# Drains of GpSimd's queue inside the program of a one-core decoder layer

## The chip, the cores and the metric

One core of one Trainium2 chip runs the whole layer. The metric is device time in microseconds (us), the median of several runs.

## The reference

A decoder layer with post-normalisation on x of 16 batches x 256 tokens x 256 features, float32. Cut to what matters:

```python
x = layernorm(x + attn(x, W_qkv, W_out))             # 16 heads, segments of 128 tokens, every 2nd key
x = layernorm(x + xattn(x, ctx, Wq, ..., Wo, bo))    # 16 heads, 77 keys of the context
logits = x @ router_w; e = argmax(logits); g = softmax(logits)[e]        # 14 experts, one per token
y = g * (gelu(x @ w1[e] + b1[e]) @ w2[e] + b2[e])
x = layernorm(x + y)
```

## The kernel before

Each engine runs a program of its own whose order is written out by hand as strings of steps (`POOL_FIRST`, `POOL_ORDER`, `POOL_LAST`, `POOL_TILES` for GpSimd and the like for the others). `step@lag` in `*_ORDER` is repeated for every two batches, `step:b` is one step of batch b, and `*_TILES` is repeated for every expert tile. Engines meet at semaphores.

The attention stage goes over the 16 batches. In it GpSimd scales the softmax's probabilities (`scale`, L1498), computes the layer norms' rstd (L1456, L1461) and masked keys (L1508, L1530), and does part of the routing. A pair of batches, p = b // 2 from 0 to 7, is 512 tokens. Once per pair, `pool_enter` writes them into the experts' lists in DRAM: four indirect DMAs of 128 entries each (L1579, "list entries"). From pair 2 on a small add to the tokens' numbers stands in front of them (L1572, "member step"), for which the first entry waits.

The expert stage goes over 45 tiles of 128 list rows. For tile j, SyncE loads the list's rows (`slots`, L722) and the expert's bias (L732), GpSimd gathers the tokens' rows by an indirect DMA (`pool_gather`, L1599, into a ring of six buffers), TensorE transposes them (`rows`, L740), makes the hidden layer (`hid`, L956) and the output (`y`, L972), VectorE adds bias (L1401) and residual (L1413) and takes statistics, GpSimd raises the variance to -0.5 (`pow`, L1613, "rs step"), VectorE normalises (L1436, "norm"), and GpSimd writes the rows to the output by an indirect DMA (`pool_put`, L1605, "put"). Tiles 0 to `NEARLY` - 1 = 10 hold tokens of the first 12 batches and start while the last batches are still in work; tiles from 11 on need the lists of all pairs.

In a steady tile the order is

```python
PE_TILES = "y@2 hid@0 rows@-1"
DVE_TILES = "eps@1 bias@0 wd@-4 res@0 stat@0 norm@1 agg@0"
POOL_TILES = "gather@-3 pow@3 put@4"
```

so that gather j is followed by pow j - 6 and put j - 7. At the change of stage `POOL_LAST` ends with `gather:6 r_less_max0:15 r_count_tile1:15 r_count_tile2:15 r_count_tile3:15 pow:0 enter0:13 gather:7 enter0:15`: the entries of pairs 6 and 7 with gather 7 between them, and behind them pow 1, put 0 and gather 8.

At the end GpSimd waits until the last four puts have landed. Then each engine's program closes with a DRAIN and a barrier of all engines, which the profile puts down to L100.

Of the kernel before, what the change touches and what calls it, by code (L numbers as in the profile page):

```python
# [48 lines left out]
def wait(eng, sig, b, k=None, held="", part=""):  # L49

    if isinstance(b, int) and b < 0 or held in HELD or f"{held}:{part}" in HELD:
        return
    eng.wait_ge(sig.sem, sig.at(b, k))


def decoder_layer(nc, x, x_cols, xk_cols, ctx_cols, w_qkv, w_out, wq, bq, wk, bk, wv, bv, wo, bo, router_w, w1, b1, w2,
# [19 lines left out]
    NTILE = NT + E - 1  # L76
# [4 lines left out]
    NEARLY = EARLY * TPB - (E - 1)  # L81
# [18 lines left out]
    with ExitStack() as top:  # L100
# [216 lines left out]
        def wait_ring(eng, ring, j, held=""):  # L317

            wait(eng, ring[j % len(ring)], j // len(ring), None, held)

        def exists(b):
            return not isinstance(b, int) or 0 <= b < B
# [238 lines left out]
        def phase_of(j):  # L561
            return int(j >= NEARLY)
# [25 lines left out]
        def settled(eng):  # L588

            eng.sem_inc(carried.sem, 1)  # L590
# [944 lines left out]
        def pool_routing(pool):  # L1535
            for what, k, b in in_order(POOL_FIRST, POOL_ORDER, POOL_LAST, POOL_TILES):
                if what == "scale":
                    pool_scale(pool, *unit_of(k, b))
                elif what == "kxblk":
                    pool_kxblk(pool, b)  # L1540
                elif what == "x1r":
                    pool_x1r(pool, b)
                elif what == "kblk":
                    pool_kblk(pool, b)
                elif what == "enter":
                    pool_enter(pool, b)
                elif what[:2] == "r_":
                    pool_route(pool, what[2:], k, b)
                elif what == "clear":
                    pool_clear(pool)  # L1550
                elif what == "gather":
                    pool_gather(pool, b)
                elif what == "put":
                    pool_put(pool, b)
                elif what == "pow":
                    pool_pow(pool, b)
                else:
                    pool_rstd(pool, int(k[0]), int(k[1]), b)

        def pool_enter(pool, b):  # L1560

            if not exists(b):
                return
            p = b // 2
            if p < 2:
                pool.sem_inc(token_stepped.sem, 1)
                pool.wait_ge(lists_filled.sem, lists_filled.at(0))
            else:
                for t in range(TPP):
                    wait(pool, entered[p % 2][t], p // 2 - 1, held="pool_enter.1", part=t)  # L1570
                settled(pool)
                nc.gpsimd.tensor_tensor(member_no[:, p % 2], member_no[:, p % 2], pair_step[:], ALU.add).then_inc(  # L1572
                    token_stepped.sem, 1)
            for t in range(TPP):
                if t == 0:
                    wait(pool, routed["place"], p, held="pool_enter.2")
                    wait(pool, routed["gate"], p, held="pool_enter.3")
                    wait(pool, token_stepped, p, held="pool_enter.4")
                nc.gpsimd.indirect_dma_start(lists, bass.IndirectOffsetOnAxis(ap=place_i[:, p % 2, t:t + 1], axis=0),  # L1579
                                             member[:, p % 2, t, :], None, bounds_check=LIST_ROWS - 1,  # L1580
                                             oob_is_err=False).then_inc(entered[p % 2][t].sem, 16)

        def pool_clear(pool):
# [2 lines left out]
                wait(pool, computed[job], B - 1)  # L1586
            nc.gpsimd.memset(xg[:].rearrange("p m d -> p (m d)"), 0.0).then_inc(rows_cleared.sem, 1)

        def pool_gather(pool, j):
            if j == 0:  # L1590
                pool.wait_ge(rows_cleared.sem, 1)
            if j in (0, NEARLY):
                for t in range(TPB):
                    for n in range(2):
                        wait(pool, x2_stored[n][t], PLANNED[phase_of(j)] // 2)
            wait(pool, f["res_done"], j - XR, held="pool_gather.1")
            wait_ring(pool, slots_loaded, j, held="pool_gather.2")
            rows = (B if phase_of(j) else EARLY) * S
            nc.gpsimd.indirect_dma_start(xg[:, j % XR, :], None, x2_dram[0:rows],  # L1599
                                         bass.IndirectOffsetOnAxis(ap=slots_no[:, j, 0:1], axis=0),  # L1600
                                         bounds_check=rows - 1, oob_is_err=False).then_inc(gathered[j % XR].sem, 16)
# [106 lines left out]
```

## Time and profile before

| | us |
|---|---|
| median of 3 runs | 639.02 (635.59 to 640.14) |
| span of the profiled execution, first to last instruction | 595.6 |
| TensorE busy in it | 563.3 (95%) |
| VectorE | 463.4 (78%) |
| ScalarE | 343.1 (58%) |
| GpSimd | 405.4 (68%) |
| GpSimd's indirect DMAs | 45 gathers, 45 puts, 32 list entries |

No time of its own is given for the profiled execution beyond its span; the median of the runs is 43.4 us above that. In the rows PE is TensorE's matmuls, DVE VectorE, ACT ScalarE, POOL GpSimd, SP SyncE; a q behind the name is the engine's queue (its sequencer), which waits and issues. A number such as L1599 is the line of the kernel. Behind an operation, in brackets, stands the idle time of its engine in front of it and what ended it; "issue" is time in which it waited for nothing that the profile shows.

### The profile page before, as it was taken

To read this page: it belongs to the slowest core of one execution; us is meant where nothing else is said; L and a number is where in the kernel's file an instruction comes from. 1 tells how busy PE (TensorE), PEld (TensorE's weight loads), DVE (VectorE), ACT (ScalarE), POOL (GpSimd) and SP (SyncE) were. 2 spreads that over 40 slices of the span, in tenths; PEclk is the share of its full clock that TensorE was granted. 3 is DMA by queue.
4 is the path that set the end of the run, shared out by engine and by line. 5 is a ranking of instruction groups with operands and counts; after the bars stand their busy time and mean duration, and the time that the engine had idled before them with its cause. 6 is when DMAs were issued, how large, how long until landed. Compare 5 with 4: busy or idle time off the path is not lost.

```text
span 595.6 us, 16640 instructions
## 1 busy us (share of the span) xinstructions
PE 563.3 (95%) x5608; PEld 476.7 (80%) x5608; DVE 463.4 (78%) x1071; ACT 343.1 (58%) x842; POOL 405.4 (68%) x554
## 2 busy tenths in 40 slices
PE   7989999999999999999999999799979999999990
PEld 6777788788888788788788778568869999999990
DVE  2779999999999899999999989865455566555561
ACT  1456666666676576665766766546625555555540
POOL 4346675678778678677678766776777677777652
PEclk9799999999999999999999999969989999999996
DMA  7415125125414314413714201114273333333200
GB/s 207 149 42 181 24 51 194 28 68 147 76 47 150 76 50 109 132 33 89 168 26 136 68 7 41 32 39 119 55 102 97 90 81 89 96 92 91 68 16 0
DMA packets 76692, 50.11 MB, mean 84 GB/s; under 512 B 39222, under 2 KB 70970, under 8 KB 76608
## 3 DMA queue, kind: packets, MB, share of 16 engines
q1 hardware_dynamic: 71264, 40.60, 26.8%
q0 software_dynamic: 5344, 8.44, 5.6%
q8 instruction: 47, 0.77, 0.6%
q14 instruction: 37, 0.30, 0.3%
HBM read 40.55 MB, written 10.60 MB: 86 GB/s over the span
## 4 chain that ended last, share of the span: by engine, by line
PE 74%; POOL 9%; issue 7%; DVE 5%; ACT 2%; DMA 1%; POOLq 0%; ACTq 0%; DVEq 0%
PE ps_r L822 15%; PE ps_r L740 13%; PE ps_s L956 10%; PE ps_r L972 10%; PE ps_r L807 5%; PE ps_r L902 5%; PE ps_s L762 4%; PE ps_s L753 3%; POOL token_lists L1579 3%; PE ps_r L795 2%; POOL prob L1498 2%; PE ps_r L879 2%; PE ps_r L897 2%; PE ps_r L904 2%; POOL out L1605 1%
## 5 line engine op out<-in xcount | busy, mean ns | idle before, releaser
L1498 POOL TENSOR_TENSOR prob<-prob,rden 128x616 f32<-128x616 f32 (+1 forms) x96 | 138.3, 1447 | 58.3 <-DVE rden L1173 56.6
L999 ACT COPY probT<-ps_r 128x512 f32<-128x512 f32 x192 | 86.8, 480 | 43.3 <-PE ps_r L740 41.4
L1141 DVE TENSOR_REDUCE mx<-ps_s 128x8 f32<-128x616 f32 (+1 forms) x96 | 88.8, 925 | 21.7 <-PE ps_s L753 14.9
L1019 ACT ACTIVATE prob<-prob 128x616 f32<-128x616 f32 (+1 forms) x96 | 79.4, 833 | 33.9 <-DVE prob L1152 33.9
L1161 DVE TENSOR_REDUCE den<-prob 128x8 f32<-128x616 f32 (+1 forms) x96 | 88.3, 921 | 6.9 <-ACT prob L1019 5.7
L1152 DVE TENSOR_TENSOR prob<-ps_s,mx 128x616 f32<-128x616 f32 (+1 forms) x96 | 89.8, 936 | 4.5 <-PE ps_r L740 3.0
L740 PE MATMUL ps_r<-ident,prob 128*128 128x128 f32 (+1 forms) x576 | 88.4, 281 | 1.6 <-POOL prob L1498 1.0
L956 PEld LDWEIGHTS ps_s<-xgT,w1b 128*128 128x128 f32 x720 | 87.2, 192 | 2.4 <-issue 0.3
L972 PE MATMUL ps_r<-w2s,hT 128*128 x360 | 86.7, 385 | 1.3 <-DVE yb L1401 1.1
L956 PE MATMUL ps_s<-xgT,w1b 128*128 128x128 f32 x720 | 87.9, 275 | 0.2 <-ACT xgT L1107 0.2
L740 PEld LDWEIGHTS ps_r<-ident,prob 128*128 128x128 f32 (+1 forms) x576 | 66.1, 142 | 16.8 <-issue 9.6
L972 PEld LDWEIGHTS ps_r<-w2s,hT 128*128 128x128 f32 x360 | 66.0, 193 | 9.3 <-issue 1.9
L1599 POOL DMA_INDIRECT xg<-x_rows,slots x45 | 47.4, 1053 | 33.8 <-DVE ys L1413 26.2
L585 DVE COPY w1b<-w1s 128x512 f32 x45 | 20.1, 447 | 55.2 <-PE ps_s L956 52.8
L1119 ACT ACTIVATE hT<-ps_s,b1t 128x128 f32<-128x128 f32 x180 | 51.4, 368 | 15.6 <-issue 12.1
L1107 ACT COPY xgT<-ps_r 128x256 f32<-128x256 f32 x45 | 16.7, 373 | 65.8 <-PE ps_r L740 65.8
L1605 POOL DMA_INDIRECT out<-yo,slots x45 | 47.4, 1053 | 8.7 <-issue 8.5
L1579 POOL DMA_INDIRECT token_lists<-member,place_i x32 | 32.4, 1013 | 13.5 <-issue 8.2
L762 PE MATMUL ps_s<-kxblk,qxT 32*128 32x154 f32 x512 | 35.2, 344 | 4.3 <-DVE prob L1152 4.3
L1461 POOL TENSOR_TENSOR rstd<-ve,neg_half 128x1 f32<-128x1 f32 x64 | 35.5, 554 | 5.0
L807 PE MATMUL ps_r<-probT,vX 128*32 128x128 f32 (+1 forms) x1024 | 37.9, 281 | 0.2 <-issue 0.2
L902 PE MATMUL ps_r<-wo_s,oTx 128*128 128x272 f32 x128 | 37.2, 414 | 0.1
(158 smaller groups left out, 1011.0 us busy)
## 6 DMA issues: line engine op xcount, KB each, us to landing
w1s<-in_w SPq DMA_DIRECT2D x14, 512.0 KB
w2s<-in_w SPq DMA_DIRECT2D x14, 512.0 KB
b2r<-in_b SPq DMA_DIRECT2D x45, 128.0 KB, 3.2
xT<-in_x_cols SPq DMA_DIRECT2D x16, 256.0 KB, 2.9
xres<-in_x SPq DMA_DIRECT2D x16, 256.0 KB
x_rows<-x2s SPq DMA_DIRECT2D x32, 128.0 KB, 1.9
xkT<-in_xk_cols SPq DMA_DIRECT2D x16, 128.0 KB, 2.7
ctxT<-in_ctx_cols SPq DMA_DIRECT2D x16, 77.0 KB, 2.1
```

The source lines that it names most:

```text
L740: return nc.tensor.transpose(dst, src, ident[:])
L807: last = nc.tensor.matmul(dst[32 * g:32 * g + 32, 0:P], vX[0:rows, b % 2, c, h, off:off + 32], probT[0:rows, par, c * P:(c + 1) * P], star ...
L822: last = nc.tensor.matmul(dst[:, 0:width], lhs(c), rhs(c), start=(c == 0), stop=(c == KC - 1))
L902: nc.tensor.matmul(dst[:, 0:DR], oTx[:, c, cols], wo_s[:, c, :], start=(c == 0), stop=False)
L956: last = nc.tensor.matmul(ps_s[:, j % 2, u * P:(u + 1) * P], w1b[:, j % 2, c, u * P:(u + 1) * P], xgT[:, j % 2, c * P:(c + 1) * P], start= ...
L972: last = nc.tensor.matmul(dst[:, 0:D], hT[:, j % 2, c, :], w2s[:, bass.ds(e, 1), c, :].rearrange("p a f -> p (a f)"), start=(c == 0), stop ...
L999: nc.scalar.copy(probT[0:rows, par, first:last], src[0:rows, 0:last - first]).then_inc(pT_copied[kind].sem, 1)
L1019: nc.scalar.activation(prob[:, n % 3, 0:width], prob[:, n % 3, 0:width], ACT.Exp, scale=SCALE).then_inc(exp_done[kind].sem, 1)
L1141: nc.vector.tensor_reduce(m, s, axis=AX, op=ALU.max).then_inc(max_done[kind].sem, 1)
L1152: nc.vector.tensor_tensor(p, s, mb, ALU.subtract).then_inc(sub_done[kind].sem, 1)
L1161: nc.vector.tensor_reduce(den[:, par, 0:heads], prob[:, n % 3, 0:heads * width].rearrange("p (h k) -> p h k", k=width), axis=AX, op=ALU.ad ...
L1498: nc.gpsimd.tensor_tensor(p, p, rden[:, par, 0:heads, None].to_broadcast([P, heads, width]), ALU.mult).then_inc(scaled[kind].sem, 1)
```

## The change

Two drains are put into GpSimd's program. One stands in front of everything that `pool_enter` does for a pair, except for pair 0: seven drains, for pairs 1 to 7. The other stands in front of the waits of a gather, for the tiles in `range(NEARLY + 4, NTILE, 6)`: gathers 15, 21, 27, 33 and 39. Nothing else is added, removed or moved.

```diff
@@ pool_enter
             p = b // 2
+            if p:
+                nc.gpsimd.drain()
             if p < 2:
                 pool.sem_inc(token_stepped.sem, 1)
@@ 
+        RETIRED_BEFORE = range(NEARLY + 4, NTILE, 6)
+
         def pool_gather(pool, j):
@@ 
                         wait(pool, x2_stored[n][t], PLANNED[phase_of(j)] // 2)
+            if j in RETIRED_BEFORE:
+                nc.gpsimd.drain()
             wait(pool, f["res_done"], j - XR, held="pool_gather.1")
```

The steps around the two drains at the change of stage, on GpSimd, in the program before (xg is the buffer of the gathers, member the tokens' numbers, token_lists the lists; the last gather of the first row is gather 6):

```order
328 L1599 DMA xg<-x2_rows,slots 128x256 x3
329 L1470 TENSOR_TENSOR ldif<-logits,lmax 128x56
330 L1487 TENSOR_TENSOR before<-before,onehot 128x14 x3
331 L1613 TENSOR_TENSOR rs<-ve,neg_half 128x1
332 L1572 TENSOR_TENSOR member<-member,pair_step 128x4
333 L1579 DMA token_lists<-member,place_i 59008x2 x4
334 L1599 DMA xg<-x2_rows,slots 128x256
335 L1572 TENSOR_TENSOR member<-member,pair_step 128x4
336 L1579 DMA token_lists<-member,place_i 59008x2 x4
337 L1613 TENSOR_TENSOR rs<-ve,neg_half 128x1
338 L1605 DMA out<-yo,slots 4096x256
339 L1599 DMA xg<-x2_rows,slots 128x256
```

In the changed program the same instructions stand in the same order on every engine. A drain, which such a list leaves out, stands in front of each of the two member steps: for pair 6 behind the rs step of tile 0, for pair 7 right behind gather 7. In the steady tiles the added drain stands between put j - 8 and gather j, once in six tiles (in front of gather 21 it is put 13).

## Rows read from the trace of the kernel before

**Rows 1.** Stretches: length, busy us and count of PE, PEld, DVE, ACT, POOL; clock, DMA, GB/s.

```profile
210.00:280.00 70.00, 69.79 (x828) 57.11 (x827) 66.95 (x140) 46.12 (x106) 52.57 (x76) 1.00 0.30 78
...
470.00:530.00 60.00, 60.00 (x419) 56.65 (x419) 36.04 (x113) 32.85 (x97) 42.83 (x49) 1.00 0.35 89
```

**Rows 2.** Last put in the timeline; POOL's queue on L100: count, min/median/max ns, starts.

```profile
585.61 0.98 POOL L1605 DMA_INDIRECT out<-yo,slots  x1 [0.30 <-issue]
...
L100 POOLq COMPARE_BRANCH  x1: 38/38/38, 587.8 to 587.8; - x1
L100 POOLq DRAIN  x1: 7417/7417/7417, 588.0 to 588.0; - x1
```

**Rows 3.** The first DRAIN of POOL's queue, on the line of the program's start.

```profile
L1697 POOLq DRAIN  x1: 171/171/171, 0.4 to 0.4; - x1
```

**Rows 4.** Groups of POOL's instructions, by line.

```profile
L1599 POOL DMA_INDIRECT xg<-x_rows,slots x45 | 47.4, 1053 | 33.8 <-DVE ys L1413 26.2 <-issue 4.6 <-DVE yo L1436 1.7
L1605 POOL DMA_INDIRECT out<-yo,slots x45 | 47.4, 1053 | 8.7 <-issue 8.5
...
L1579 POOL DMA_INDIRECT token_lists<-member,place_i x32 | 32.4, 1013 | 13.5 <-issue 8.2 <-POOL member L1572 5.2
```

**Rows 5.** Timeline of pair 2: start, length, operation [idle before]; POOL, then PE.

```profile
235.36 0.20 POOL L1572 TENSOR_TENSOR member<-member,pair_step 128x4 uint32<-128x4 uint32 x1
236.43 1.07 POOL L1579 DMA_INDIRECT token_lists<-member,place_i  x1 [0.87 <-POOL member L1572]
...
241.35 1.24 POOL L1498 TENSOR_TENSOR prob<-prob,rden 128x616 f32<-128x616 f32 x1
...
242.73 0.74 PE L740 MATMUL ps_r<-ident,prob 128*128 128x128 f32 x5 [0.19 <-POOL prob L1498]
```

**Rows 6.** Timeline of pair 1: POOL, then PE.

```profile
188.76 1.16 POOL L1579 DMA_INDIRECT token_lists<-member,place_i  x1 [0.39 <-issue]
...
193.82 1.24 POOL L1498 TENSOR_TENSOR prob<-prob,rden 128x616 f32<-128x616 f32 x1
...
195.36 0.49 PE L740 MATMUL ps_r<-ident,prob 128*128 128x128 f32 x3
```

**Rows 7.** Timeline, POOL, behind the entries of pair 5.

```profile
387.48 1.21 POOL L1498 TENSOR_TENSOR prob<-prob,rden 128x616 f32<-128x616 f32 x1 [1.70 <-DVE rden L1173]
```

**Rows 8.** Timeline, POOL: gather 6 and member step, gather 7 and member step, gather 8.

```profile
412.08 1.00 POOL L1599 DMA_INDIRECT xg<-x_rows,slots  x1 [1.45 <-DVE ys L1413]
...
414.65 0.19 POOL L1572 TENSOR_TENSOR member<-member,pair_step 128x4 uint32<-128x4 uint32 x1
...
421.13 1.27 POOL L1599 DMA_INDIRECT xg<-x_rows,slots  x1 [0.30 <-issue]
422.42 0.27 POOL L1572 TENSOR_TENSOR member<-member,pair_step 128x4 uint32<-128x4 uint32 x1
...
430.54 1.04 POOL L1599 DMA_INDIRECT xg<-x_rows,slots  x1 [0.30 <-issue]
```

**Rows 9.** From issue to landing, L1599: gather 6, gather 7, gather 8.

```profile
DMA to landing us min/median/max: 2.8/2.8/2.8
...
DMA to landing us min/median/max: 5.8/5.8/5.8
...
DMA to landing us min/median/max: 7.0/7.0/7.0
```

**Rows 10.** Timeline, PE, around gather 8's landing.

```profile
437.58 0.66 PE L740 MATMUL ps_r<-ident,xg 128*128 128x128 f32 x2 [3.50 <-DMA xg<-x_rows,slots]
438.03 3.39 PE L972 MATMUL ps_r<-w2s,hT 128*128 x8
```

**Rows 11.** Gather 21 on POOL and its landing; norm 15 on DVE; PE takes gather 21.

```profile
478.63 1.05 POOL L1599 DMA_INDIRECT xg<-x_rows,slots  x1 [0.62 <-issue]
...
DMA to landing us min/median/max: 3.6/3.6/3.6
...
481.88 0.40 DVE L1436 TENSOR_SCALAR yo<-ys,mv,rs 128x256 f32<-128x256 f32 x1
...
487.83 0.38 PE L740 MATMUL ps_r<-ident,xg 128*128 128x128 f32 x2
```

## The prediction

> **What bounds the kernel now.** I read the views in this order: busy time by stage, the last instructions of the program, the instruction groups of GpSimd, GpSimd's order of time at the places of the added drains with TensorE's waits beside it, and the chain around the change of stage. In the attention stage TensorE is busy 69.79 of 70 us, and in the steady expert stage 60.00 of 60 [rows 1]: it has no idle time to lose, so a delay there costs nothing until it reaches TensorE, and then costs its full length. The program doesn't end with work. The last put is issued at 585.61; GpSimd has seen the last landing when its branch stands at 587.8, and then a DRAIN on its queue takes 7.417 us before the cores' closing barrier [rows 2]. Between the stages, GpSimd is the chain: gathers, list entries, and gather 8, for which TensorE idles 3.50 us up to 437.58 [rows 8 to 10].
>
> **What a drain costs.** Before the final drain 45 gathers, 45 puts and 32 list entries were issued [rows 4]: 122 indirect DMAs, all landed. The program's first GpSimd DRAIN, with no DMA behind it, took 0.171 us [rows 3]. I read the difference as bookkeeping per DMA not yet retired: 7.417/122 = 0.061 us each. That is a choice; the trace has one such drain, and the ends are 0 and the whole 7.417 us whatever the count. The Trainium skill, in "VectorE: DVE Perf Modes", section "The DRAIN you can't avoid", tells of boilerplate drains of about 12 ns on all engines. By that rule both the added drains and what they could save would be nothing and the time stay 639; GpSimd's 171 and 7417 ns [rows 2, 3] go against it.
>
> The change adds 12 drains: one ahead of the entries of pairs 1 to 7, and one ahead of gathers 15, 21, 27, 33 and 39. Counted in program order they find 4, 4, 4, 4, 4, 11, 5, then 19, 12, 12, 12 and 12 entries (103 together) and leave 19 (gathers 39 to 44, puts 32 to 44) for the last one.
>
> **The last drain** falls from 122 x 0.061 to 19 x 0.061: -6.3 us, all on the end. Ends: 0 and -7.2.
>
> **Pairs 1 to 5.** The entries of the pair before were issued some 48 us earlier (188.76 and 236.43) [rows 5, 6] and have long landed, so a drain costs 4 x 0.061 + at most 0.17 + about 0.1 to start again = 0.5 us of GpSimd, which also loses its reading ahead. For pairs 2 to 4 this is on the path: behind the member step (235.36) come four entries and then the scaling at 241.35 [rows 5], and TensorE waits 0.19 us for just that scaling. Pairs 3 and 4 stand the same: 3 x 0.5 = 1.5. In pair 1 there is no member step, so the first entry DMA is prepared ahead; behind a drain it would come as late as behind the member step, 0.87 us [rows 5], so about 0.4 more, 0.9. The scaling there ends at 193.82 + 1.24 = 195.06 and TensorE takes it at 195.36 [rows 6]; a scaling ended at 242.59 was taken at 242.73, so some 0.15 is slack: 0.75. In pair 5 GpSimd idles 1.70 us before the next scaling [rows 7], which hides 0.5; without that cover it would be 0.5 more. Sum +2.2; ends 0 and 4 (twice the drain).
>
> **Pairs 6 and 7**, the expensive part. Gather 6 starts at 412.08 and lands 2.8 us later, at 414.9 [rows 8, 9]. The drain of pair 6 stands where the member step stood, 414.65. It waits for that landing, if a drain waits for landings, and does 11 entries (0.67): between 415.0 and 415.6, say +0.7. The drain of pair 7 stands right behind gather 7, issued at 421.13 and landing 5.8 us later at 426.9, while the member step now starts at 422.42 [rows 8, 9]. With pair 6's shift: 426.9 + 0.7 + 5 entries (0.3) = 427.9. So the member step and all queued behind it (four entries, the rs step of tile 1, put 0, gather 8) start 5.5 us later, and gather 8 at 430.54 + 5.5 = 436.0. VectorE's norm of tile 1 waits for the rs step, its bias step of tile 3 stands behind that norm, and y of tile 5 behind the bias: all 5.5 late, but TensorE needs gather 8 only after them. Gather 8 took 7.0 us to land [rows 9]. The drained queue may make that shorter: gather 7, behind one group of entries, took 5.8, gather 6 with none 2.8. So TensorE resumes between 436.0 + 2.8 = 438.8 and 443.0, against 437.54: +1.3 to +5.5. I take +5.5, as put 0, the bias rows and the second group of entries, which stand in front of or beside gather 8, move with it. A longer idle stretch may also lengthen the slow clock behind it: the y matmuls at 438.03 took 3.39 us [rows 10], some 1.5 more than those of the tiles after; one more such piece would be another 1.5 us. I leave that to the range.
>
> Of waiting for landings the trace shows nothing: its one long drain began when all had landed. From the rows the wait is between 0 and the 4.5 us from 422.4 to 426.9. I choose the wait, since a drain that costs by DMA has to look at each DMA. The Trainium skill, in "Perfetto Trace Analysis", section "DMA Instruction — SWDGE (GPSIMD)", says that such an instruction is over when its descriptors are written, before the data moves. If a drain waits only for instructions, that gives the second rival below.
>
> **Gathers 15 to 39.** Each drain stands behind a put just issued. Take gather 21: the put before it ends at 478.0 (0.62 idle before 478.63) and lands by about 479.2 to 480.6 (the last put needed at most 1.2 us behind its end at 586.6 [rows 2], gather 21 2.6, 3.6 less 1.05), and 12 entries take 0.7, partly beside the waiting. Gather 21 starts near 480.9 rather than 478.63. It would land at 484.5 against TensorE's use at 487.83 [rows 11]: 3.3 us are left of 5.6. The rs step behind it is some 2.3 late, the norm at 481.88 [rows 11] about 0.8, and VectorE works it off in its idle time. GpSimd idles 33.8 + 8.7 us before 45 gathers and puts [rows 4], 0.9 per tile, and a tile is 3.73 us (419 matmuls in 60 us [rows 1], 26 to a tile), so it is back in step after three tiles and the next drain comes after six. Cost 0; if the cover failed, the excess over 5.6 us, five times. High end +3.
>
> **The sum**, against the profiled span of 595.6: +2.2 + 5.5 + 0 - 6.3 = +1.4. The median of the runs, 639.0, is 43.4 above the span; I take what lies around it as unchanged. Forecast 640.4.
>
> **Rivals.**
> - The last drain doesn't shrink (slower). It is one mechanism, in the closing drain: it costs its 7.4 us whatever was retired before, for instance because it resets the queue, while the others cost what I give. Then +2.2 + 5.5 = +7.7, 646.7. For it: only one observation of 7.4 us. Against it: nothing had to be waited for, and 122 divides into a plausible step. It decides as soon as less than 1.3 us of the 6.3 comes back.
> - A drain doesn't wait for landings (faster, inside 1%). Pairs 6 and 7 then cost only 0.8 + 0.4 = 1.2: 2.2 + 1.2 - 6.3 = -2.9, 636.1.
> - A drain goes over all earlier DMAs, retired or not: 4, 8, 12, 16, 20, 31, 36, 55, 67, 79, 91, 103 of them. Pairs 1 to 4 cost 2.4 + 0.6, pairs 6 and 7 about 7, the late ones up to 6.3 us, just hidden, and the last stays: +10, 649.
> - A fixed 7.4 us per drain: four on the path in the attention stage alone make 30 us, the others some 35 more: about 700. Against it: the 0.171 us drain.
> - Faster by over 1%: the drained queue lets gather 8 land at 2.8 us (-4.2), and more than the drain shrinks at the end.
>
> **Chances.** Forecast 0.62, its own range 637 to 644; no waiting 0.14; last drain unchanged 0.10; all DMAs 0.07; fixed 0.03; faster 0.04. A measurement of this kernel tells about 1% (6.4 us) from no change. Slower by over 1%: 0.07 + 0.03 + 0.07 of the third case = 0.17; faster 0.05 with the edge of the no-waiting case; within 0.78. Range 635 to 647: the low end is the no-waiting case with 1 us to spare, the high one the unchanged last drain.
>
> **What would show it.** Right: the closing DRAIN about 1.2 us; drains of pairs 2 to 5 near 0.3 to 0.5 us; the one of pair 7 about 4.5 to 5 us long and ending with gather 7's landing; gather 8 issued near 438 (with the attention stage's 2.2) and TensorE's wait for it longer than 3.5 us; tiles at 3.73 us throughout. Wrong: a closing drain of 7 us, drain lengths that grow from pair to pair, a member step of pair 7 that follows its gather at once, or TensorE waits for gathers after 450.

## The result and the profile after

The changed kernel took 628.63 us (median of 6 runs, 624.13 to 629.51), the one before 636.35 (6 runs, 633.35 to 640.14, the three of the table before among them): ratio 0.9875, 95% interval 0.9838 to 0.9911. It is 1.2% faster, by 7.7 us between these medians. The forecast was 640.4, no change. Two of the executions profiled below were slower than most of their kernel's own runs (e5's, 632.17 us against a median of 626.98, and e8's, 635.19 against 630.39), so means of stages leave them out.

One plain fact has to stand ahead of everything else. In every profiled run whose own time is known, time and span differ by 1.7 to 1.8 us: here 628.91 and 627.1, for the kernel before, run again later, 635.47 and 633.7 in one session and 594.83 and 593.1 in another. So the 43.4 us between the span of 595.6 and the median of 639.02 never lay around the program. The profile shown before and the runs shown beside it come from **two kinds of session**: one in which the kernel before takes 593 to 595 us, and one in which it takes 634 to 639. One and the same chip gave both, in different sets of runs. To read the changed kernel's profile one needs the kernel before in the same kind, so here it is the copy of experiment e6.

The changed kernel's span is 627.1 us at a mean granted clock of 0.949, e6's 633.7 at 0.939. The same four stretches of both: up to VectorE's bias step of tile 0, from there to that of tile 10, to that of tile 44, and to the end. Columns as in [rows 1]. The changed kernel:

```profile
0.00:442.10 442.10, 410.72 (x4473) 331.84 (x4474) 359.61 (x736) 251.51 (x581) 281.68 (x411) 0.94 0.30 82
442.10:494.00 51.90, 43.80 (x285) 39.87 (x284) 25.79 (x94) 24.10 (x66) 33.54 (x41) 0.93 0.44 76
494.00:618.60 124.60, 124.32 (x855) 116.29 (x853) 76.11 (x236) 66.01 (x196) 91.33 (x98) 1.00 0.31 78
618.60:627.10 8.50, 0.00 (x0) 0.00 (x0) 2.32 (x8) 0.00 (x0) 4.28 (x5) 0.63 0.01 0
```

The kernel before (e6):

```profile
0.00:450.20 450.20, 417.82 (x4473) 336.41 (x4474) 360.08 (x736) 251.32 (x581) 281.39 (x411) 0.93 0.30 81
450.20:494.90 44.70, 40.70 (x279) 36.96 (x278) 25.39 (x94) 24.06 (x66) 33.75 (x42) 1.00 0.41 88
494.90:619.40 124.50, 124.22 (x860) 116.72 (x858) 75.07 (x237) 66.63 (x196) 86.31 (x98) 1.00 0.30 78
619.40:633.70 14.30, 0.00 (x0) 0.00 (x0) 2.28 (x8) 0.00 (x0) 4.28 (x5) 0.57 0.01 0
```

Stage by stage: -8.1, +7.2, +0.1, -5.8; sum -6.6, the difference of the spans. The last two were forecast (0 and -6.3), the second in kind (+5.5), the first not at all (+2.2). The work is the same in it (4473 matmuls recorded), but TensorE's busy time fell by 7 us at a slightly higher clock: part of it had run at half speed.

**Answer to [rows 1].** The stretch of the attention stage in the changed kernel's own trace:

```profile
210.00:280.00 70.00, 66.80 (x772) 53.83 (x774) 60.42 (x122) 42.02 (x97) 44.97 (x62) 0.95 0.27 68
```

The attention stage is no longer without idle time and at full clock, as it was in [rows 1]. This is the session's doing, not the change's: the copy of the kernel before shows it too (66.00 us busy in the same 70, clock 0.93). Its waits, TensorE's list of waits in e6 (us in total, times, longest):

```profile
PE ps_r L902 <- ACT oTx L1012: 16.6, 5, 3.8
```

Once per pair of batches, for pairs 0 to 4, TensorE stops for up to 3.8 us at L902, and around the end of each stop a stretch of 6.8 to 10.2 us at half its clock (1.2 GHz) begins. Period of two batches in e6 from the third stop on: 54.7 us (254.30 to 309.00). The periods of e1, where there is no such stop, are 46.65. Five times 8 us is the 40 us between the two kinds.

**Answer to [rows 2] and [rows 3].** The drains of the changed kernel, by line (count, min/median/max ns, first and last start): list entries, gathers, closing one.

```profile
L1566 POOLq DRAIN  x7: 981/1003/9584, 191.9 to 450.9; - x7
...
L1601 POOLq DRAIN  x5: 5151/5812/6397, 490.4 to 582.6; - x5
...
L100 POOLq DRAIN  x1: 1598/1598/1598, 625.3 to 625.3; - x1
```

The closing one fell from 7417 to 1598 ns. An added drain's record begins while GpSimd is still at the instructions ahead of it, so its length isn't its price. At pair 3 the price is the 0.52 us in front of the member step; there was none before:

```profile
299.54 0.20 POOL L1574 TENSOR_TENSOR member<-member,pair_step 128x4 uint32<-128x4 uint32 x1 [0.52 <-issue]
300.61 1.07 POOL L1581 DMA_INDIRECT token_lists<-member,place_i  x1 [0.87 <-POOL member L1574]
...
304.55 0.97 POOL L1581 DMA_INDIRECT token_lists<-member,place_i  x1 [0.30 <-issue]
...
497.52 1.05 POOL L1605 DMA_INDIRECT xg<-x_rows,slots  x1 [3.88 <-issue]
```

The last row is gather 15, held up 3.88 us by its drain, and no TensorE wait answers to it.

**Answer to [rows 8] and [rows 10].** Pair 7 in the changed kernel: gather 7, the member step, gather 8; then VectorE's norm of tile 1, and TensorE's y of tile 5.

```profile
454.09 1.05 POOL L1605 DMA_INDIRECT xg<-x_rows,slots  x1 [0.30 <-issue]
460.62 0.19 POOL L1574 TENSOR_TENSOR member<-member,pair_step 128x4 uint32<-128x4 uint32 x1 [5.47 <-issue]
...
468.67 1.04 POOL L1605 DMA_INDIRECT xg<-x_rows,slots  x1 [0.30 <-issue]
...
467.19 0.47 DVE L1436 TENSOR_SCALAR yo<-ys,mv,rs 128x256 f32<-128x256 f32 x1 [9.28 <-POOL rs L1619]
...
468.43 3.78 PE L972 MATMUL ps_r<-w2s,hT 128*128 x8 [5.73 <-DVE yb L1401]
```

The member step follows its gather after 5.47 us instead of at once. The rs step behind the entries comes late, VectorE waits 9.28 us for it, its bias step stands behind that norm, and TensorE stops 5.73 us for the bias, then works its y at 3.78 us for eight matmuls instead of the 1.89 of the tile before: half clock (granted from 467.2 to 474.0).

### The profile page after: what moved, and what is told of

It is laid out like the page before. It is cut to its first block, busy times and chain, and to the rows that moved or that the text cites. A ratio compares the mean times of both kernels' runs of the same rounds, so it can differ in the third digit from the quotient of the medians.

```text
span 627.1 us, 16645 instructions
## 1 busy us (share of the span) xinstructions
PE 578.8 (92%) x5608; PEld 488.0 (78%) x5608; DVE 463.8 (74%) x1071; ACT 341.6 (54%) x842; POOL 410.8 (66%) x554
## 4 chain that ended last, share of the span: by engine, by line
PE 58%; issue 15%; POOL 11%; DVE 6%; DMA 2%; another core or an unknown queue 2%; ACT 2%; POOLq 1%; SPq 1%; DVEq 0%; ACTq 0%
PE ps_r L822 15%; PE ps_r L740 12%; PE ps_r L807 6%; PE ps_r L902 5%; PE ps_s L762 4%; POOL out L1611 4%; PE ps_s L753 4%; POOL rs L1619 3%; POOL xg L1605 3%; PE ps_r L795 2%; PE ps_r L879 2%; PE ps_r L897 2%; PE ps_r L904 2%; DVE prob L1152 1%
## 5 line engine op out<-in xcount | busy, mean ns | idle before, releaser
L740 PE MATMUL ps_r<-ident,prob 128*128 128x128 f32 (+1 forms) x576 | 90.6, 286 | 1.9 <-POOL prob L1498 1.3
L956 PEld LDWEIGHTS ps_s<-xgT,w1b 128*128 128x128 f32 x720 | 88.1, 194 | 5.4 <-issue 3.1
L956 PE MATMUL ps_s<-xgT,w1b 128*128 128x128 f32 x720 | 88.9, 277 | 2.6 <-ACT xgT L1107 2.6
L740 PEld LDWEIGHTS ps_r<-ident,prob 128*128 128x128 f32 (+1 forms) x576 | 68.5, 146 | 17.1 <-issue 9.8
L1605 POOL DMA_INDIRECT xg<-x_rows,slots x45 | 49.0, 1090 | 31.7 <-issue 27.1
L902 PE MATMUL ps_r<-wo_s,oTx 128*128 128x272 f32 x128 | 40.7, 445 | 17.0 <-ACT oTx L1012 13.3
L1611 POOL DMA_INDIRECT out<-yo,slots x45 | 50.6, 1124 | 8.4 <-issue 8.3
L1436 DVE TENSOR_SCALAR yo<-ys,mv,rs 128x256 f32<-128x256 f32 x45 | 19.3, 429 | 47.7 <-POOL rs L1619 47.7
L902 PEld LDWEIGHTS ps_r<-wo_s,oTx 128*128 128x128 f32 x128 | 24.1, 209 | 23.3 <-ACT oTx L1012 15.3
L807 PE MATMUL ps_r<-probT,vX 128*32 128x128 f32 (+1 forms) x1024 | 40.3, 293 | 0.6 <-ACT probT L999 0.4
```

Source lines behind the costliest of these rows:

```text
L740: return nc.tensor.transpose(dst, src, ident[:])
L807: last = nc.tensor.matmul(dst[32 * g:32 * g + 32, 0:P], vX[0:rows, b % 2, c, h, off:off + 32], probT[0:rows, par, c * P:(c + 1) * P], star ...
L902: nc.tensor.matmul(dst[:, 0:DR], oTx[:, c, cols], wo_s[:, c, :], start=(c == 0), stop=False)
L956: last = nc.tensor.matmul(ps_s[:, j % 2, u * P:(u + 1) * P], w1b[:, j % 2, c, u * P:(u + 1) * P], xgT[:, j % 2, c * P:(c + 1) * P], start= ...
```

## The experiments

Eighteen experiments. The kind of session could not be chosen; each experiment names the kind that it got. "With stops" is the kind of e6, "without" that of the trace shown before the change.

**e1 and e6: the kernel before, unchanged.** No diff.

> The kernel before, unchanged, profiled once more. What it is for: the changed kernel's span is 627.1 us and its time 1.8 more, while the kernel before has a span of 595.6 and a median of 636 to 639. Theory A (what lies around the span isn't fixed: the program before leaves 122 indirect DMAs to be retired, and that costs some 40 us behind the last instruction): span near 596, time near 637. Theory B (the profiled execution of before was not like its timed ones; the stalls of 3 to 4 us of TensorE once per pair, seen in the changed kernel, are in the kernel before as well): span near 635, with five such stalls, time 2 above it.

e1 fell without stops: 593.62 us against 593.71, ratio 1.0003 (0.9968 to 1.0038). Its profiled execution took 594.83 with a span of 593.1, so nothing like 40 us lies behind the span: theory A is out.

> The kernel before once more, for its profile on this chip. If this chip is like the one of the first result (median of before 636): TensorE's stalls of 3 to 4 us beside the entries of pairs 0 to 4, as in the changed kernel's profile there. If it is like that of the first four runs: span near 593 and none of them.

e6 fell with stops: 635.47, span 633.7. Here the missing 40 us showed: inside the span and in the attention stage.

**e5, e7, e17: the changed kernel again.** No diff.

> The changed kernel itself, beside the kernel before on one chip. On the chip of the first four runs the parts added up to nothing: the pairs' drains +6.3 us, the tiles' drains -6.2. Theory A (the gain of 1.2% that was measured belongs to the chip or session in which both kernels took 40 us more): here, if the kernel before takes 594, the changed one takes 593 to 595, ratio 0.998 to 1.003. Theory B (the parts interact, and the gain is the kernel's own): ratio near 0.988, 587.

> The changed kernel once more, on whatever chip. Two kinds of session were seen: one in which the kernel before takes 594 us and TensorE never waits more than 1 us at its output-projection reads of the attention stage, and one in which it takes 634 to 636 us and TensorE waits 3 to 4 us once per pair of batches there. Theory (parts add): on the first kind tiles' drains -6.0, drains of pairs 1 to 6 about +4, pair 7's about +3, sum -0.5 to +2, ratio 1.00; on the second kind 0.988 as measured twice. Rival: the gain of 1.2% is the same on both kinds: 0.988 on the first kind too.

> The changed kernel as measure of the same call for the two kernels before it: 0.9886 of before again on the slower kind, 1.00 (0.998 to 1.004) on the faster one.

With stops 0.9886 (0.9849 to 0.9923) and 0.9886 (0.9845 to 0.9927), without stops 1.0029 (1.0002 to 1.0057), 595.32 against 593.16. The gain belongs to the sessions with stops: that was theory A of e5, and e7's rival is out. The stretches of e17, without stops, bounded as above:

```profile
0.00:410.30 410.30, 394.52 (x4473) 319.49 (x4474) 362.75 (x736) 251.73 (x581) 281.38 (x411) 0.98 0.32 88
410.30:460.40 50.10, 42.65 (x277) 39.14 (x276) 26.31 (x95) 24.20 (x66) 33.64 (x41) 0.90 0.42 81
460.40:585.20 124.80, 124.56 (x862) 116.99 (x860) 76.29 (x236) 66.05 (x196) 91.82 (x98) 1.00 0.30 78
585.20:593.70 8.50, 0.00 (x0) 0.00 (x0) 2.33 (x8) 0.00 (x0) 4.28 (x5) 0.69 0.01 0
```

and of the kernel before in that kind (e1):

```profile
0.00:408.80 408.80, 395.77 (x4473) 320.73 (x4474) 360.48 (x735) 252.04 (x581) 281.15 (x411) 0.98 0.33 89
408.80:453.90 45.10, 41.47 (x277) 37.96 (x276) 25.54 (x94) 24.01 (x66) 33.76 (x42) 0.96 0.42 90
453.90:578.80 124.90, 124.64 (x864) 117.14 (x862) 75.03 (x237) 66.73 (x197) 86.14 (x98) 1.00 0.29 77
578.80:593.10 14.30, 0.00 (x0) 0.00 (x0) 2.30 (x8) 0.00 (x0) 4.28 (x5) 0.62 0.01 1
```

+1.5, +5.0, -0.1, -5.8: the forecast's terms were +2.2, +5.5, 0, -6.3. In the kind of session in which the profile had been taken, each term comes near what was forecast. Pair 7 in e17, gather 7 and member step, then y of tile 5 and the rows of gather 8 on TensorE:

```profile
422.29 1.07 POOL L1605 DMA_INDIRECT xg<-x_rows,slots  x1 [0.30 <-issue]
428.44 0.19 POOL L1574 TENSOR_TENSOR member<-member,pair_step 128x4 uint32<-128x4 uint32 x1 [5.08 <-issue]
...
436.25 3.77 PE L972 MATMUL ps_r<-w2s,hT 128*128 x8 [6.82 <-DVE yb L1401]
...
443.00 0.44 PE L740 MATMUL ps_r<-ident,xg 128*128 128x128 f32 x2 [0.32 <-DMA xg<-x_rows,slots]
```

The size is right and the place is not: not the wait for gather 8 grew (0.32 us; 2.30 in e1), the wait for the bias step did (6.82; 1.06 in e1).

**e2 and e16: the pairs' drains alone.**

```diff
+            if p:
+                nc.gpsimd.drain()
```

> Only the seven drains ahead of the list entries. They cost about 1.0 us each and 9.6 in pair 7 in the changed kernel's profile. If the gain comes from them: 628 to 630, ratio 0.988. If they only cost: above 637, up to 645, with a closing drain of about 5 us (90 entries left).

> Only the seven drains of the pairs, this time with luck on the slower kind of session; on the faster kind it was 1.0106 of before. Theory (parts add: changed 0.9886, tiles only 0.9937): 0.995 on the slower kind, with TensorE's waits at pairs 2 to 4 at 3.2 us and the stretches at half clock behind them at 6.8 us instead of 10.2, and the closing drain at 7.07. Rival: the shorter stretches need the tiles' drains or come by chance: time as before or 1% above.

Both fell without stops: 1.0106 (1.0065 to 1.0147) and 1.013 (1.0074 to 1.0185), so 6 to 8 us slower. What they do by themselves in a session with stops was not seen.

**e3 and e8: the gathers' drains alone.**

```diff
+            if j in RETIRED_BEFORE:
+                nc.gpsimd.drain()
```

> Only the five drains ahead of gathers 15 to 39. If the gain comes from the shorter closing drain and the late drains are hidden: about 631 to 633 (some 6 us less than before). If the late drains of 5 to 6 us each reach TensorE: 637 or more.

> Only the five drains in front of gathers 15 to 39. Theory: the gain is the shorter closing drain (7.42 to 1.60 us, -5.8) on either kind of session: -5 to -6 us. On the second kind the changed kernel's attention stage was about 3 us shorter as well, so there this kernel should lose that part and keep TensorE's waits of 3.6 us and the 10.2 us stretches at half clock as before. Rival: drains in the tiles cost something where TensorE is already slower: -3 or less.

e3, without stops: 587.67 us, 0.9888 (0.9848 to 0.9927), the fastest kernel of that kind. e8, with stops: 0.9937 (0.9893 to 0.9981), -4.0 us, between its theory and its rival, and the interval holds both. Both close with the drain of 1598 ns. In e8 TensorE's stops are those of the kernel before, the half-clock stretches 10.2 us each, and the attention stage ends at 452.2, no earlier than in e6 (450.2): the gain of the first stage doesn't come from the gathers' drains.

**e4 and e9: without pair 7's drain.**

```diff
-            if p:
+            if p and p != 7:
                 nc.gpsimd.drain()
```

(e4 also lacked one wait of VectorE at pair 7, on a signal that pair 0 had already given.)

> The changed kernel without the one drain of pair 7 that waits 9.6 us for gather 7 and the entries in front of it. If that wait is fully exposed, as forecast: 5 to 9 us faster than the changed kernel, 620 to 624. If it is covered by something else in the timed executions: 628.

> All added drains but the one of pair 7 (12 less 1). Theory: pair 7's drain delays the rs step of tile 1, the norm and the output matmuls of the expert stage (TensorE waits 5 us there in the changed kernel), part of it caught up: 2 to 4 us faster than the changed kernel of the same call, about -10 us against before on the second kind, -2 to -4 on the first. Rival: the wait only moves one that stands a few us later, and the two kernels are within 1 us.

e4, without stops: 591.82, 0.9962 (0.9937 to 0.9987). e9, with stops: 0.9918 (0.9883 to 0.9952), not the 2 to 4 us ahead of the changed kernel that were expected; the two can't be told apart. Its tiles 0 to 10 did take less, 47.9 us against 49.6 in e7 of the same session, but in place of the 5.0 us for the bias step TensorE has a stop of 5.0 us at L956 that the profile puts down to nothing. That stop isn't e9's alone: e8, e10, e11, e12 and e13, all with stops and without pair 7's drain, have one of 3.5 to 3.6 us at L956 near pair 7's entries; e6 has none over 2.2. What makes it is open.

**e10: one drain alone, at gather 39.**

```diff
-        RETIRED_BEFORE = range(NEARLY + 4, NTILE, 6)
+        RETIRED_BEFORE = (39,)
```

> One drain alone, in front of gather 39. It finds 32 list entries, 39 gathers and about 32 puts before it. Theory (the closing drain's length goes by the number of DMAs since the last drain, and never counts more than some 90): the one drain takes 7 to 9 us beside work that hides it, the closing drain is 1.60 us as with five, and the time is that of the tiles-only kernel within 1 us. Rival 1: a drain this long is not hidden any more, TensorE waits 2 us or more behind gather 39: gain 4 us or less. Rival 2: several drains are needed to clear everything, and the closing drain stays over 3 us.

With stops, 0.9987 (0.9934 to 1.0039). Gather 39 behind the drain, and TensorE's rows:

```profile
597.08 1.05 POOL L1603 DMA_INDIRECT xg<-x_rows,slots  x1 [9.36 <-issue]
...
599.30 0.44 PE L740 MATMUL ps_r<-ident,xg 128*128 128x128 f32 x2 [1.31 <-DMA xg<-x_rows,slots]
```

One drain clears the queue as well as five do (closing drain 1608 ns), but GpSimd stands 9.36 us for it, more than the cover of a gather; tiles 10 to 44 take 126.9 us (124.5 in e6). Rival 1 is right in kind, that it isn't hidden (1.31 us of wait rather than 2, 2.4 us of stage), and about the small gain as far as its wide interval goes. Spread over five places the drains cost 0 to 1.2 us together (below).

**e11: a different edit for each pair**, on the kernel before.

```diff
+                if p == 2 and t:
+                    nc.gpsimd.drain()
+                n = 16 if p == 1 or (p == 3 and t) else P
-                nc.gpsimd.indirect_dma_start(lists, bass.IndirectOffsetOnAxis(ap=place_i[:, p % 2, t:t + 1], axis=0),
-                                             member[:, p % 2, t, :], None, bounds_check=LIST_ROWS - 1,
+                nc.gpsimd.indirect_dma_start(lists, bass.IndirectOffsetOnAxis(ap=place_i[:n, p % 2, t:t + 1], axis=0),
+                                             member[:n, p % 2, t, :], None, bounds_check=LIST_ROWS - 1,
+            if p == 4:
+                nc.gpsimd.drain()
```

> The kernel before, with a different edit for each pair: pair 1's four entries are cut to 16 rows each (its other tokens are not entered), pair 2 has a drain between its entries, pair 3 keeps its first entry whole and cuts the other three to 16 rows, pair 4 has a drain behind its last entry. Looked at in a session in which TensorE waits 3 to 4 us once per pair in the attention stage. Theory (the entries' own DMAs hold TensorE up, by the rows that they write): pair 1's wait goes (under 0.7 us), pair 3's falls to about a third, pair 2's is spread or smaller, pair 4's is as before, 3.6 to 3.8. Rival (the wait belongs to something else that falls at the same time): all five waits stay within 1.8 to 3.8 us as before.

With stops (642.54 us, one run). Pair 2's entries with drains between them, and TensorE at pair 1, whose entries had 16 rows:

```profile
258.08 0.98 POOL L1582 DMA_INDIRECT token_lists<-member,place_i  x1 [7.33 <-issue]
262.74 0.97 POOL L1582 DMA_INDIRECT token_lists<-member,place_i  x1 [3.68 <-issue]
```

```profile
198.90 0.27 PE L807 MATMUL ps_r<-probT,vX 104*32 104x128 f32 x1 [1.03 <-issue]
```

Two readings. First, a drain right behind a DMA costs several us (7.33 and 3.68 of idle GpSimd): it waits for the landing, which the trace shown before the change could not tell. In the trace's records of the landing signals, the last one of the entry in front comes at 256.86, 261.87 and 266.68, and the drains end at 257.27, 261.96 and 266.76: 0.41 us behind where nine DMAs are to be retired (eight entries of pairs 0 and 1 are among them), 0.09 and 0.08 behind where it is one. The drain of pair 7 does the same: its end comes 0.24 us behind gather 7's last landing signal in all six profiles that have it (428.30 and 428.06 in e17). Second, cutting the rows did not simply remove the stops. At pair 1 the stop broke up into three small ones (0.33 to 1.03 us) between the attend matmuls while the entries were being issued (194.6 to 199.05), and one of 0.79 us behind them; at pair 3, with one whole entry and three of 16 rows, the stop was 3.59 us, at pair 4 3.52. The theory of a price by rows falls; so does its rival, by pair 1.

**e14 and e18: cut entries and a single drain.**

> The kernel before with all four list entries of pair 2 cut to 16 rows each and those of pair 4 to 64 rows each (the other tokens are not entered); pairs 0, 1 and 3 as before. The run of four cut entries at pair 1 left a wait of 1.0 us there, and one whole entry ahead of three cut ones at pair 3 left the whole 3.6 us, so a price by rows alone is out. Theory (the first entry's full DMA brings the wait, whatever follows): pair 2 has no wait over 1.1 us, pair 4's is as before or somewhat less, 2 to 3.8 us. Rival (the wait is not the entries' doing, pair 1 only happened to be small, as it is small in the kernel before, 1.8 us): pair 2's is 3 us or more.

> The kernel before with the four list entries of pair 2 cut to 16 rows each and one added drain, in front of pair 3's entries; pairs 0, 1 and 4 as before. It tells something of TensorE's waits only in a session that has them. There, theory (the entries bring the wait, the drain shortens it and the half-clock stretch behind it by itself): pair 2 under 1.1 us, pair 3 at 3.2 us with 6.8 us at half clock, pair 4 back at 3.6 to 3.8 us with 10.2. Rival (what shortens them is the drains of the pairs or tiles as a whole, or the phase between engines): pair 3 as pair 4. In a session without such waits: a time within 3 us of before.

```diff
@@ e14, entries [:n] as in e11
+                n = {2: 16, 4: 64}.get(p, P)
@@ e18, entries [:n] as in e11
+            if p == 3:
+                nc.gpsimd.drain()
+                n = 16 if p == 2 else P
```

Both fell without stops (592.02 and 591.76, one run each) and told nothing of them. e18 gave a point on the closing drain instead, below.

**e12: adds in place of the drains** of pairs 1 to 6; none at the gathers.

```diff
+            if p and p != 7:
+                for n in range(2):
+                    nc.gpsimd.tensor_tensor(idle_pad[:, 2 * p + n], pair_step[:], pair_step[:], ALU.add)
```

> The kernel before, and in front of the list entries of pairs 1 to 6 two small adds of GpSimd into a tensor of their own (0.2 us each, with the gap between them about as long as the drain there takes, 0.4 to 0.5 us); no drain. Theory A (the drain shortens TensorE's waits only by moving the entries 0.5 us against TensorE's work): on the slower kind of session the periods of pairs 2 to 4 are 52.4 to 53.2 us as with drains, against 54.7 to 54.9, and the time is 3 to 6 us below before. Theory B (it does so by what it retires): the periods stay at 54.7 to 55, and the time is that of before or 1 to 2 us above.

With stops, 0.9977 (0.9934 to 1.002); periods from the second stop on 55.2, 54.9, 54.8. At pair 3 the two adds, the last entry, and TensorE's stop (TensorE's and ScalarE's lines are 1 higher, the entries' 4):

```profile
305.87 0.40 POOL L1568 TENSOR_TENSOR idle_pad<-pair_step 128x4 uint32<-128x4 uint32 x2
307.21 1.09 PE L808 MATMUL ps_r<-probT,vX 128*32 128x128 f32 x32
307.28 1.07 POOL L1583 DMA_INDIRECT token_lists<-member,place_i  x1 [0.87 <-POOL member L1576]
...
311.31 0.97 POOL L1583 DMA_INDIRECT token_lists<-member,place_i  x1 [0.30 <-issue]
...
313.55 1.70 PE L903 MATMUL ps_r<-wo_s,oTx 128*128 128x272 f32 x3 [4.56 <-ACT oTx L1013]
```

The stop grew to 4.56 us and ended 1.27 us behind the last entry, as without adds. The numbers are those of theory B, but they don't exclude theory A, because the adds moved the entries less than the drains do. Against the start of TensorE's attend matmuls (L807, here L808) the first entry of pairs 2 to 4 stands at -0.27 us in e6 and at +0.08 in e12, but at +0.30 with the drains.

**e13: pair 0 too.**

```diff
-            if p and p != 7:
+            if p != 7:
                 nc.gpsimd.drain()
```

> The kernel with all added drains but pair 7's, and a drain in front of pair 0's entries as well. If a drain ahead of the entries shortens the half-clock stretch behind TensorE's wait, period 0 to 1 is 1 to 2 us shorter than the 54 us of the others and the time is 1 to 2 us below that kernel's (0.990 of before on the slower kind). Rival: at pair 0 nothing is to be retired, and nothing changes (within 1 us).

With stops, 0.9895 (0.9825 to 0.9966). The first period is 53.9 us, within the others' 53.3 to 55.1: the rival, nothing changes in it.

**e15: pairs 2 to 5 and the gathers.**

```diff
-            if p:
+            if 2 <= p <= 5:
                 nc.gpsimd.drain()
```

> The changed kernel without the drains of pairs 1, 6 and 7. By the stages seen so far the drains of pairs 2 to 5 and of the tiles carry all of the gain, pair 7's costs 3 us at the start of the expert stage, pair 1's and pair 6's nothing or up to 1 us. Theory: on the slower kind of session about 3 us faster than the changed kernel, 0.983 to 0.988 of before. Rival (what pair 7's drain costs is caught up in the later tiles, as the kernel without it was not measurably faster than the changed one): within 1 us of the changed kernel, 0.989.

Without stops: 590.51, 0.9955 (0.993 to 0.9981), against 1.0029 for the changed kernel (e17) of the same session: 4.8 us faster, so what pair 7's drain costs, with those of pairs 1 and 6, is not caught up there. It beats both kernels in this kind of session; e3 beat it further. In the other kind it was not timed.

## Why the prediction was wrong

**The step that failed** is "I take what lies around it as unchanged", about the 43.4 us between span and median. The note in the text that the sum is made against the profiled span was right; that the rest lies around the program was not. It lay in it, as TensorE's stops in the attention stage, in sessions of which the trace at hand had none. By that the term "Pairs 1 to 5", +2.2 us, was priced on a path that the timed runs didn't have. What they had in its place is a first stage shorter by 7.7 us: the mean of four profiles with the pairs' drains (bias step of tile 0 at 442.1 in the changed kernel, 441.4 in e7, 442.9 in e9, 445.7 in e13) less that of three without (450.2 in e6, 450.7 in e10, 451.4 in e12). The two left out fall in the same way (e5 446.7, e8 452.2), and no value of one group reaches the other. The pairs' drains alone were never timed in a session with stops.

**What the pairs' drains did there.** At pair 3 of e6 and of the changed kernel (its entries stand above): TensorE's attend matmuls (L807), the entries, ScalarE's two copies of their result, and TensorE's resumption at L902. First e6:

```profile
302.80 1.07 POOL L1579 DMA_INDIRECT token_lists<-member,place_i  x1 [0.87 <-POOL member L1572]
303.07 1.09 PE L807 MATMUL ps_r<-probT,vX 128*32 128x128 f32 x32
306.36 0.27 ACT L1012 COPY oTx<-ps_r 128x128 f32<-128x128 f32 x1 [2.25 <-remote]
306.74 0.97 POOL L1579 DMA_INDIRECT token_lists<-member,place_i  x1 [0.30 <-issue]
308.59 0.27 ACT L1012 COPY oTx<-ps_r 128x128 f32<-128x128 f32 x1 [1.96 <-remote]
309.00 1.25 PE L902 MATMUL ps_r<-wo_s,oTx 128*128 128x272 f32 x2 [3.79 <-ACT oTx L1012]
```

Then the changed kernel:

```profile
300.32 1.09 PE L807 MATMUL ps_r<-probT,vX 128*32 128x128 f32 x32
...
305.29 1.16 PE L902 MATMUL ps_r<-wo_s,oTx 128*128 128x272 f32 x4 [3.18 <-ACT oTx L1012]
```

The rows put the stop down to ScalarE's copy, but ScalarE itself is waiting. What it waits for ("remote" in the rows) is the semaphore of the attend matmuls, whose rows end by 304.16: the trace's record of its two updates has 306.34 and 308.57. The transposes (L740) behind them, which end at 305.21 by their rows, give their signal at 308.66. At the same place of e1 such signals come within 0.06 us of the rows' ends, and VectorE's and ScalarE's do so in e6 as well. The ends in TensorE's rows are modelled; by the signals it was held up inside the attends and transposes, while the entries were being issued.

In e6 TensorE goes on 1.29 us behind the end of the last entry (307.71). So it does at every pair from 0 to 4 of the four undrained profiles with stops: 1.1 to 1.5 us behind it, 20 times of 20. In the changed kernel it goes on at 305.29, 0.23 us ahead of the last entry's end (305.52); so at pairs 2 to 4 of all five profiles with the pairs' drains, 0.1 to 0.9 us ahead, 15 of 15. What comes one entry earlier is the attends' second signal (304.85); the transposes' is still held until 306.31, 0.8 us behind the last entry. At pair 1 the drain doesn't bring this (0.4 us behind once, 1.2 four times). The stretch at half clock was at pairs 2 to 4 mostly 6.8 us or less (13 of 15) instead of 10.2. Together:

```profile
254.30:309.00 54.70, 50.70 (x548) 40.93 (x549) 44.21 (x89) 30.63 (x72) 34.63 (x48) 0.91 0.29 80
```

```profile
252.85:305.29 52.44, 49.24 (x549) 39.98 (x549) 44.06 (x89) 30.70 (x71) 34.67 (x49) 0.94 0.29 81
```

54.70 to 52.44 us for the same work: 0.6 us less of a stop (3.79 to 3.18), and 1.5 less of TensorE's busy time (50.70 to 49.24), about what 3.4 us at 1.2 instead of 2.4 GHz cost. That the stops are tied to the issue of the entries is what these ends and e11's small steps show.

**Retiring or shifting?** The two can be told apart to a degree by where the first entry starts against the attends:

| first entry less first attend, us | where | stop, us | L902 against the last entry's end, us |
|---|---|---|---|
| -0.92, -0.78 | pair 1 without a drain (-0.78 in e12) | 1.8 to 2.3 | +1.4 to +1.5 |
| -0.78 | pair 0 | 3.0 to 3.8 | +1.1 to +1.3 |
| -0.27 | pairs 2 to 4 without drains | 3.5 to 3.8 | +1.2 to +1.4 |
| -0.15 | pair 0 with a drain (e13) | 4.3 | +1.2 |
| +0.08 | pairs 2 to 4 of e12 (adds) | 4.6 | +1.3 |
| +0.08 | pair 1 with a drain | 4.5 to 4.6, once 3.7 | +1.2 to +1.3, once +0.4 |
| +0.30 | pairs 2 to 4 with drains | 2.6 to 3.3 | -0.1 to -0.9 |

Adds and a drain that put the entries at the same place leave the same stop, though the drain retires four entries and the adds none. At pair 1 of e7, beside e12's rows above:

```profile
193.46 1.09 PE L807 MATMUL ps_r<-probT,vX 128*32 128x128 f32 x32
193.54 1.07 POOL L1581 DMA_INDIRECT token_lists<-member,place_i  x1 [1.38 <-POOLq L1566]
...
199.77 1.24 PE L902 MATMUL ps_r<-wo_s,oTx 128*128 128x272 f32 x3 [4.53 <-ACT oTx L1012]
```

So the shift of the entries is the likelier cause, and e12 stopped some 0.2 us short of the place where it pays. It isn't shown: no run put the entries at +0.30 without a drain. Nor does any run show why TensorE is held up while GpSimd issues DMAs, and why in some sessions only. e8 and e10 exclude the gathers' drains; drains of pairs without those of the gathers ran three times (e2, e16, e18), each time where there are no stops.

**Term by term**, without stops, where the terms were worked out (means of the profiles with and without each edit, e14 and e18 left out for their cut entries):
- Last drain: -5.8 instead of -6.3. The mechanism was right and the size per DMA off. The closing drain took 1598 ns for 19 entries, 7070 for 86 (e2), 8377 for 102 (e11), 9040 for 110 (e18): 0.082 us per entry, straight through all four. The forecast's 0.061 divided 7417 by 122; by the line, 7417 is 90 entries. That the term came out near is luck: a price too low by a quarter times a count too high (103 for 71). If the line holds there, some 32 of the 122 had been retired without a drain; what retired them stays open.

```profile
L100 POOLq DRAIN  x1: 8377/8377/8377, 632.1 to 632.1; - x1
```

```profile
L100 POOLq DRAIN  x1: 9040/9040/9040, 580.8 to 580.8; - x1
```

- Pairs 1 to 5: forecast +2.2. The starts of the tiles (409.7 with the drains, 407.9 without) can't carry this term, as those without lie between 404.6 and 410.2, with a half-clock stretch of 3.4 to 13.7 us near 385. Counted on TensorE from pair 0's L902 to pair 5's (143.03 to 376.16 in e1), it is 233.1, 233.1 and 233.9 us without the pairs' drains and 235.6 to 236.5 in e2, e4, e16 and e17: +2.6. At pair 2 of e17 TensorE's wait for the scaling went from 0.20 (e1) to 0.77 us, 0.57 for the 0.5 of the forecast.
- Pairs 6 and 7: +4.4 (49.5 against 45.1 for tiles 0 to 10; 49.2 to 50.1 with pair 7's drain, 43.8 to 46.3 without), forecast +5.5. The choice that a drain waits for landings was right (e11, and the end 0.24 us behind gather 7's landing). The second rival, no waiting, is out. The words on where TensorE would feel it were wrong: "TensorE needs gather 8 only after them" leaves out that it needs the bias step itself, for y of tile 5.
- Gathers 15 to 39: 0, measured +0.5 for tiles 10 to 44 (124.8 to 126.0 in four profiles with the drains, 124.7 to 124.9 in four without), -0.1 in e17. GpSimd's idle time at gather 21 went from 0.61 (e1) to 2.78 us (e17), +2.2 for the forecast's 2.3; at gather 15 it was 4.0 to 6.1. The cover mostly held that too: TensorE waited for a gather 0.43 us once in e3 and 0.91 once in e15, and not in e4 or e17.
- With the terms as measured the sum is +2.6 + 4.4 + 0.5 - 5.8 = +1.7, and e17's runs found +1.7 (0.1 to 3.4); the forecast's +1.4 is of that size because its errors cancel (+2.2, +5.5, 0, -6.3).

**The other rivals.** An unchanged last drain, a drain over all earlier DMAs and 7.4 us per drain fall with the 1598 ns and with drains of pairs 1 to 4 that all record 0.98 to 1.00 us. The Trainium skill's 12 ns for boilerplate drains ("VectorE: DVE Perf Modes", "The DRAIN you can't avoid") does not hold for GpSimd: 1598 ns with 19 DMAs un-retired. The other engines' first drains (7 to 10 ns in the kernel before) agree with it, their closing ones (123 to 1507 ns) don't. The Trainium skill's word that such a DMA instruction is over when the descriptors are written ("Perfetto Trace Analysis", "DMA Instruction — SWDGE (GPSIMD)") agrees with the trace (gather 6's row is 1.00 us long, its landing 2.8 us behind its start), but the drain behind it waits for the data: 7.33 us in e11.

**With stops** the ledger is -7.7 (first stage), +3.7 (tiles 0 to 10: 50.8 in two profiles against 47.1 in three), +0.2, -5.8: -9.6, where the ratios of the three timings come to -7 to -8; the rest is within the scatter of single profiles (tiles 0 to 10 alone take 44.7 to 48.6 without the pairs' drains).

## What to carry to other kernels

Before a prediction is built on a profile, hold its span against the times of the runs: a gap of 7% is not "around" the program, it says that the profile was taken under other conditions, and that terms may act which it doesn't show. GpSimd's closing drain costs by the indirect DMAs that no drain has retired yet (0.08 us each here): drains of a dozen entries each, spread where GpSimd has slack, took that off the end for 0 to 1.2 us. One right behind a DMA on a path that others wait for is dear: it waits for the landing, and everything queued behind it waits too. And when a dummy operation stands in for a drain to test a shift, measure the shift it makes: e12's was 0.35 us where the drain's was 0.57.

## What was not expected of the hardware

- The same program on the same chip ran in 593 us in one session and 636 in another, all of the difference in five periods of the attention stage, each with a stop of TensorE of up to 3.8 us that ends with the issue of GpSimd's list entries and a stretch of up to 10.2 us at 1.2 GHz around its end.
- In those stops TensorE's rows look finished and its signals aren't given: in e6 they came up to 4.4 us behind the rows' modelled ends, so that the profile puts the stop down to ScalarE, which was waiting for TensorE.
- A change can lose in one kind of session and win in the other: the changed kernel is at 1.0029 and at 0.9886, the gathers' drains alone at 0.9888 and 0.9937. A judgement from one session would have picked a different kernel.
- A drain's length is a straight line over the entries that it finds (0.082 us each, from 19 to 110), except that the 122 of the kernel before count as 90. Behind a landing that it had to wait for it takes less: 0.24 us with five, 0.41 with nine.
